# P.V. of four cross-attention heads in 512 columns, and the rotated queries turned one step earlier, in a decoder layer

## The reference

```python
scores = jnp.einsum('bqhgd,bkhd->bhgqk', q, k) * scale
attn = jax.nn.softmax(scores.astype(jnp.float32), axis=-1).astype(q.dtype)
out = jnp.einsum('bhgqk,bkhd->bqhgd', attn, v)
return out.reshape(b, q_len, N_HEADS * HEAD_DIM) @ Wo
```

## Time and profile before

| | us |
|---|---|
| median of 3 runs (1052.87 to 1053.89) | 1053.47 |
| the profiled execution | 1053.37 |
| its span | 1051.7 |
| TensorE busy | 1027.2 |
| DVE busy | 645.4 |
| ACT busy | 544.2 |
| POOL busy | 385.5 |

### The profile page before, as it was taken

How to read it: one execution, slowest core, us unless ns; L and a number is a source line. 1 busy time by engine, 2 the same in 40 slices (tenths; PEclk the granted TensorE clock), 3 DMA queues, 4 the chain that set the end, 5 groups by cost and what they waited for, 6 DMA issues and landing times.

```text
span 1051.7 us, 18418 instructions
## 1 busy us (share of the span) xinstructions
PE 1027.2 (98%) x6808; PEld 916.8 (87%) x6808; DVE 645.4 (61%) x1369; ACT 544.2 (52%) x1657; POOL 385.5 (37%) x370
## 2 busy tenths in 40 slices
PE   6999999999999999999999999999999999999997
PEld 5677777777889999999999999999999999799996
DVE  6788888887436555546545556555555575556554
ACT  5666666666526555536445446455545456522111
POOL 3544544544235324316224325225234236511110
PEclk9999999999999999999999999999999999999999
DMA  8300111105652003112022111121211013200000
GB/s 327 115 28 21 34 41 42 41 21 141 175 162 82 25 31 112 61 41 61 21 79 63 63 45 55 50 61 51 81 51 51 31 61 122 74 7 20 20 21 21
DMA packets 70114, 68.53 MB, mean 65 GB/s; under 512 B 3984, under 2 KB 53904, under 8 KB 70032
## 3 DMA queue, kind: packets, MB, share of 16 engines
q1 hardware_dynamic: 70032, 67.43, 20.5%
HBM read 48.55 MB, written 18.87 MB: 64 GB/s over the span
## 4 chain that ended last, share of the span: by engine, by line
PE 92%; DVE 4%; ACT 2%; issue 1%; DMA 1%; SPq 0%; POOLq 0%; POOL 0%; DVEq 0%; ACTq 0%
PE bank L218 27%; PE bank L220 26%; PE bank L219 26%; PE bank L945 5%; PE bank L729 2%; PE bank L689 1%; PE bank L693 1%; PE bank L699 1%; ACT Pb L1192 1%; DVE b_nb L1545 1%; PE bank L696 1%; DVE b_max L1542 1%; PE bank L611 1%; DMA rawKV<-in_L_attn_Wv_dram 1%; DVE PTal L1304 0%
## 5 line engine op out<-in xcount | busy, mean ns | idle before, releaser
L548 POOL TENSOR_TENSOR Pb<-Pb,b_rec 128x512 f32<-128x512 f32 x128 | 133.1, 1040 | 353.1 <-DVE b_rec L1549 352.7
L218 PE MATMUL bank<-XTh,WQh 128*128 128x256 f32 x512 | 145.9, 285 | 2.5 <-DVE Ql L1304 2.4
L220 PE MATMUL bank<-XTh,WQl 128*128 128x256 f32 x512 | 144.9, 283 | 0.0
L219 PE MATMUL bank<-XTl,WQh 128*128 128x256 f32 x512 | 144.8, 283 | 0.0
L1192 ACT ACTIVATE Pb<-bank,b_nb 128x256 f32<-128x256 f32 x256 | 119.0, 470 | 40.8 <-DVE b_nb L1545 40.1
L1304 DVE TENSOR_TENSOR Ol<-bank,Oh 128x256 fp32r<-128x256 f32 x128 | 54.0, 422 | 116.0 <-ACT Oh L1055 113.8
L1055 ACT ACTIVATE PTh<-bank 128x512 fp32r<-128x512 f32 x128 | 76.7, 599 | 85.3 <-PE bank L945 85.1
L1110 ACT ACTIVATE Pa<-bank,a_nb 128x128 f32<-128x128 f32 x256 | 90.4, 367 | 44.8 <-DVE a_nb L1425 44.8
L218 PE MATMUL bank<-WOh,Oh 128*128 128x512 f32 x256 | 110.0, 430 | 1.2 <-DVE x_res L1559 1.2
L510 POOL TENSOR_TENSOR Pa<-Pa,a_rec 128x512 f32<-128x512 f32 x64 | 68.2, 1066 | 104.6 <-DVE a_rec L1431 104.0
L218 PEld LDWEIGHTS bank<-XTh,WQh 128*128 128x128 f32 x512 | 97.7, 191 | 8.8 <-DVE Ql L1304 4.1
(11 more groups left out here) (230 smaller groups left out, 2865.0 us busy)
## 6 DMA issues: line engine op xcount, KB each, us to landing
kv_scratch<-KVst SPq DMA_DIRECT2D x64, 256.0 KB, 3.1
KV<-kv_scratch SPq DMA_DIRECT2D x32, 512.0 KB, 3.5
raw<-in_L_xattn_Wo_dram SPq DMA_DIRECT2D x32, 256.0 KB, 3.3
raw<-in_L_xattn_Wq_dram SPq DMA_DIRECT2D x24, 256.0 KB, 4.3
cx<-in_ctx_dram SPq DMA_DIRECT2D x8, 256.0 KB, 9.2
raw_first<-in_L_xattn_Wq_dram SPq DMA_DIRECT2D x8, 256.0 KB, 4.8
raw<-in_L_ffn_up_w_dram SPq DMA_DIRECT2D x8, 256.0 KB, 3.6
raw<-in_L_ffn_down_w_dram SPq DMA_DIRECT2D x8, 256.0 KB, 2.6
```

What stands on the lines that cost most here:

```text
L218: pe.matmul(dst, lh, rh, start=start, stop=False)
L219: pe.matmul(dst, lh, rl, start=False, stop=False)
L220: return pe.matmul(dst, ll, rh, start=False, stop=stop)
L548: gp.tensor_tensor(pk, pk, b_rec[:, k % 4, :].unsqueeze(2).to_broadcast([P, 2, KEYS]), ALU.mult).then_inc(b_g_norm, 1)
```

## The change

Cross-attention: `outputs` handles a quad, the two duos of an even and the following odd step (`QUADS` = 16 in a group, `QB` = 2 in a batch). `PTh` and `PTl` are laid out by key chunk, each with 512 columns of four heads. P.V. of a quad stands in the next even step between the scores and the transposes, and that of the last quad where P.V. of duo 31 stood. It waits for `PTl` of the quad's odd duo and for `Ol` of the quad before. ACT and DVE empty the whole bank 5 once per quad, at the beginning of the even step: ACT ahead of `PTh`, DVE behind the maxima and ahead of `PTl`. The counts that SP, `out_piece` and ACT's weight chunks wait for are changed to quads.

Self-attention: `turn_qk`, `qk_hi` and `qk_lo` are split. The queries' part stands in step 6 (on TensorE behind the transposes of step 6 and ahead of `values(5)`, on ACT and DVE at the end of step 6), the keys' part stays in step 7.

```diff
@@ SP group
-                            sp.wait_ge(b_pe_pv, DUOS * g + done)
+                            sp.wait_ge(b_pe_pv, QUADS * g + done // 2)
@@ TensorE
-            def turn_qk(b):
-
-                pe.wait_ge(v_qr, 2 * b + 2)
+            def turn_q(b):
+
+                pe.wait_ge(v_qr, 2 * b + 1)
...
+            def turn_k(b):
+
+                pe.wait_ge(v_qr, 2 * b + 2)
@@ TensorE batch
+                    if j == 6 and not last:
+                        turn_q(b + 1)
                     if j == 7 and not last:
-                        turn_qk(b + 1)
+                        turn_k(b + 1)
@@ TensorE out_piece
-                pe.wait_ge(b_v_o, DUOS * g + PB * b + i + 2)
+                pe.wait_ge(b_v_o, QUADS * g + QB * b + i // 2 + 2)
@@ TensorE outputs
-            def outputs(g, k):
-
-                pe.wait_ge(b_v_pt, DUOS * g + k + 3)
-                pe.wait_ge(b_v_o, DUOS * g + k + 1)
-                slot = (k // PB) % 3
+            def outputs(g, q):
+
+                pe.wait_ge(b_v_pt, DUOS * g + 2 * q + 4)
+                pe.wait_ge(b_v_o, QUADS * g + q + 1)
+                slot = (q // QB) % 3
                 for c in range(2):
...
-                    op = split3(pe, bank[5][:, 0:KEYS], vh, vl, PTh[:, k % 2, c * KEYS:(c + 1) * KEYS],
-                                PTl[:, k % 2, c * KEYS:(c + 1) * KEYS], c == 0, c == 1)
+                    op = split3(pe, bank[5][:], vh, vl, PTh[:, c, :], PTl[:, c, :], c == 0, c == 1)
@@ TensorE group
+                    if k and k % 2 == 0:
+                        outputs(g, k // 2 - 1)
 
                     pe.wait_ge(b_g_norm, DUOS * g + k + 1)
...
-                    if k:
-                        outputs(g, k - 1)
                 out_piece(g, NB - 1, 0)
-                outputs(g, DUOS - 1)
+                outputs(g, QUADS - 1)
@@ ACT batch
+                    if j == 6 and not last:
+                        q_hi(b + 1)
                 if not last:
-                    qk_hi(b + 1)
+                    k_hi(b + 1)
@@ ACT outputs
-                hi(Oh[:, b % 2, 2 * i:2 * i + 2, :],
-                   bank[5][:, 0:KEYS].rearrange("p (h n) -> p h n", h=2)).then_inc(b_a_o, 1)
+                hi(Oh[:, b % 2, 4 * i:4 * i + 4, :],
+                   bank[5][:].rearrange("p (h n) -> p h n", h=4)).then_inc(b_a_o, 1)
@@ ACT group
                 for k in range(DUOS):
-
+                    if k and k % 2 == 0:
+                        outputs(g, k // 2 - 1)
                     act.wait_ge(b_pe_pt, DUOS * g + k + 1)
-                    hi(PTh[:, k % 2, :], bank[3 + k % 2][:]).then_inc(b_a_pt, 1)
+                    hi(PTh[:, :, (k % 2) * KEYS:(k % 2 + 1) * KEYS],
+                       bank[3 + k % 2][:].rearrange("p (c n) -> p c n", c=2)).then_inc(b_a_pt, 1)
@@ DVE batch
+                    if j == 6:
+                        q_lo(b + 1)
                 if not last:
-                    qk_lo(b + 1)
+                    k_lo(b + 1)
@@ DVE group
+                    if k and k % 2 == 0:
+                        outputs(g, k // 2 - 1)
                     dve.wait_ge(b_a_pt, DUOS * g + k + 1)
-                    lo(PTl[:, k % 2, :], bank[3 + k % 2][:], PTh[:, k % 2, :]).then_inc(b_v_pt, 1)
+                    cols = slice((k % 2) * KEYS, (k % 2 + 1) * KEYS)
+                    lo(PTl[:, :, cols], bank[3 + k % 2][:].rearrange("p (c n) -> p c n", c=2),
+                       PTh[:, :, cols]).then_inc(b_v_pt, 1)
...
-                    if k:
-                        outputs(g, k - 1)
```

More of the change, by code:

```diff
@@ L52 @@
 PB = XG // 2
+QUADS = DUOS // 2
+QB = PB // 2
 INT, LAT, NE = 1024, 256, 8
@@ L832, in _ @@
             turn_weights(6)
-            turn_qk(0)
+            turn_q(0)
+            turn_k(0)
             unit(0, (2, 3))
@@ L1076, in values_hi, with q_hi, k_hi @@
                    bank[0][:, P:2 * P].rearrange("p (j d) -> p j d", j=SKV)).then_inc(a_v, 1)
-            def qk_hi(b):
+            def q_hi(b):
                 act.wait_ge(pe_qk, 2 * b + 1)
                 hi(QTh[:], bank[1][:].rearrange("p (k n) -> p k n", k=KC)).then_inc(a_qk, 1)
+            def k_hi(b):
                 act.wait_ge(pe_qk, 2 * b + 2)
@@ L1163, in _ @@
             weight_a(6)
-            qk_hi(0)
+            q_hi(0)
+            k_hi(0)
             act.wait_ge(v_c, 2)
@@ L1220, in _, with outputs @@
             hi(GTh[:, :, 0:NE], gate_raw[:]).then_inc(c_a_g, 1)
-            def outputs(g, k):
-                act.wait_ge(b_pe_pv, DUOS * g + k + 1)
-                if g == 0 and k == 0:
+            def outputs(g, q):
+                act.wait_ge(b_pe_pv, QUADS * g + q + 1)
+                if g == 0 and q == 0:
                     for slot in range(SLOTS):
                         act.wait_ge(st_u[slot], stored_in(slot, NU))
-                b, i = k // PB, k % PB
-                hi(Oh[:, b % 2, 2 * i:2 * i + 2, :],
-                   bank[5][:, 0:KEYS].rearrange("p (h n) -> p h n", h=2)).then_inc(b_a_o, 1)
+                b, i = q // QB, q % QB
+                hi(Oh[:, b % 2, 4 * i:4 * i + 4, :],
+                   bank[5][:].rearrange("p (h n) -> p h n", h=4)).then_inc(b_a_o, 1)
             def group(g, last):
@@ L1245, in split_weights @@
                             elif i == NUP + NFC:
-                                act.wait_ge(b_pe_pv, DUOS * g + 24)
+                                act.wait_ge(b_pe_pv, QUADS * g + 12)
                             else:
@@ L1389, in values_lo, with q_lo, k_lo @@
                 lo(vv[0], bank[0][:, P:2 * P].rearrange("p (j d) -> p j d", j=SKV), vv[1]).then_inc(v_vl, 1)
-            def qk_lo(b):
+            def q_lo(b):
                 dve.wait_ge(a_qk, 2 * b + 1)
                 lo(QTl[:], bank[1][:].rearrange("p (k n) -> p k n", k=KC), QTh[:]).then_inc(v_qkl, 1)
+            def k_lo(b):
                 dve.wait_ge(a_qk, 2 * b + 2)
@@ L1515, in _ @@
             weight_a(6)
-            qk_lo(0)
+            q_lo(0)
+            k_lo(0)
             dve.wait_ge(g_const, 9)
@@ L1593, in _, with outputs @@
             lo(GTl[:, :, 0:NE], gate_raw[:], GTh[:, :, 0:NE]).then_inc(c_v_g0, 1)
-            def outputs(g, k):
-                dve.wait_ge(b_a_o, DUOS * g + k + 1)
-                if g == 0 and k == 0:
+            def outputs(g, q):
+                dve.wait_ge(b_a_o, QUADS * g + q + 1)
+                if g == 0 and q == 0:
                     for slot in range(SLOTS):
                         dve.wait_ge(st_u[slot], stored_in(slot, NU))
-                b, i = k // PB, k % PB
-                lo(Ol[:, b % 2, 2 * i:2 * i + 2, :], bank[5][:, 0:KEYS].rearrange("p (h n) -> p h n", h=2),
-                   Oh[:, b % 2, 2 * i:2 * i + 2, :]).then_inc(b_v_o, 1)
+                b, i = q // QB, q % QB
+                lo(Ol[:, b % 2, 4 * i:4 * i + 4, :], bank[5][:].rearrange("p (h n) -> p h n", h=4),
+                   Oh[:, b % 2, 4 * i:4 * i + 4, :]).then_inc(b_v_o, 1)
             def group(g, last):
```

## The result

| | before | changed |
|---|---|---|
| median, us | 1053.43 | 1045.84 |
| range of 4 runs, us | 1052.87 to 1053.89 | 1045.18 to 1046.71 |
| the profiled execution, us | 1053.37 | 1046.71 |
| its span, us | 1051.7 | 1045.0 |

The account below looks back on a forecast made before the run. TensorE, busy 98% of the span, was taken to bound the kernel. Terms 3.4 + 2.1 - 0.9 + 1.7 + 3.1 = 9.4 us off 1053.4 gave 1044.0; term bounds 1041.8 to 1047.5, range with rivals 1041.5 to 1049.5.

Parts of the forecast that it names:

- P.V. in 512 columns: Cross-attention P.V. on TensorE: a pair takes 1.38 us instead of 1.44, over 64 pairs; 3.4 us gained.
- group starts: Cross-attention steps 0 to 3 of each group: TensorE's stall in step 2 shrinks from 0.80 to 0.29; 2.1 us gained.
- group ends: First three cross-attention groups: output piece 2 waits 0.3 us for the last P.V.'s low part; 0.9 us lost.
- last group from step 24: Last cross-attention group, where no Q remains: TensorE's standing falls from 3.0 to 1.3 us; 1.7 us gained.
- queries in step 6: Seven self-attention batches with a successor: query transposes fill TensorE's wait after T(6); 0.44 us each, 3.1 us gained.
- The Trainium skill's two prices: For P.V. matmuls: a gap formula gives 15 ns a pair, 1 us in all; sustained 131 ns would give 42 us.
- The wait for PTl in the steady steps: Cross-attention P.V. waiting for the odd duo's PTl: forecast not to occur, PTl ready 1.6 us after T, cover some 3.6.
- The slower rival: Steady cross-attention steps: PTl of the odd duo is late, 56 pairs standing 0.25 us cost 14, giving 1058; chance 0.05.
- The three waits for the low part of the output bank: Last group from step 24: TensorE waits like the 0.6 us around 906.25, forecast to go.
- the new 1.1 before the last batch's first piece: Last group, behind out of step 31: the next out waits for the residual, forecast at 1.0 us.
- the waits only move: Rival: cross-attention group starts and last group give nothing, group ends cost their 0.9; 1047.8 us, chance 0.17.
- TensorE's hole: Self-attention batch end: T(6) done at 119.35, values product starts only at 119.88 for PTal; query transposes should fill it.

Follow-up runs that it names:

- e3: The changed kernel with P.V. of a quad as 4 times 3 matmuls of 256 columns in place of 2 times 3 of 512; 1048.61 us.
- e4: The changed kernel with P.V. of each group's last quad ahead of the last batch's first output piece instead of behind it; 1043.85 us.
- e2: The kernel before with only the self-attention edits, the rotated queries in step 6; 1049.95 us.
- e6: The changed kernel without b_nb: maximum negated in the reduction, score scale put into the key weights at the start; 1047.78 us.
- e9: The changed kernel with each group's last P.V. before the output piece and no b_nb, score scale in the key products' copy out of the bank; 1041.18 us.
- e7: The changed kernel with only TensorE's query transposes in step 6, ACT's QTh and DVE's QTl behind step 7 again; 1048.86 us.

## Why the prediction was right or wrong

The time, 1045.84, lies within the forecast's own range of 1041.8 to 1047.5; the gain of 7.6 is 1.8 short of 9.4. (The slow end of that range was added up wrongly: the lowest values that the terms were given, 3.0, 1.2, -1.2, 0.9 and 0, make 3.9 us and 1049.5.) Term by term:

| term | forecast, us | measured, us | from |
|---|---|---|---|
| P.V. in 512 columns | 3.4 | 2.9 | 1.440 and 1.394 a pair, x 64; e3 |
| group starts | 2.1 | 1.7 | distances of steps 0 to 3 |
| group ends | -0.9 | -0.96 | 3 x 0.32; e4 |
| last group from step 24 | 1.7 | 0.25 | stalls of 2.98 before, 2.74 after |
| queries in step 6 | 3.1 | 3.0 | 7 x 0.42; e2 |

- **P.V. width.** The mechanism was right; the distance from start to start is 0.232 in this place, not the 0.230 of the stretch in the earlier trace rows. The Trainium skill's two prices (TensorE: Matmul & The Clock Gate, Back-to-back issue gap) do not hold for these matmuls: where its formula makes 15 ns a pair, the rows have 46.
- **The wait for PTl in the steady steps.** It did not appear: steps alternate between 3.99 and 5.37 us, 9.36 a pair where it was 9.41. The slower rival is out.
- **Group starts.** Second to fourth group as walked: the stall of 0.80 went, and P.V. of step 2 stands 0.21 and 0.10. In the first group a second one appeared that the walk had not: step 4 stands 0.35 because b_nb of step 3 ran 1.27 us behind a POOL weight part. So the 0.6 forecast for that group became 0.2.
- **The last group.** This is the term that failed. The three waits for the low part of the output bank and the 1.3 for the residual did go, and the new 1.1 before the last batch's first piece came as forecast (1.27 in place of 0.23). But at step 30, where 0.3 was written, stand 1.16, and 0.46 at step 26, where nothing was. Both are PTl behind a blocked b_nb; the walk had put POOL's weight parts elsewhere by some tenths. The rival "the waits only move" was therefore right for the last group (2.98 against 2.74) and wrong for the group starts. e6 and e9 show the cause by taking the operation away: 3.2 us in cross-attention, 1.3 of it in the last group, where 1.45 were missing.
- **Queries in step 6.** Right in size, and its reasons hold: values(6) came forward, 0.18 and 0.10 were given back at values(7) (0.15 to 0.25 forecast), and the projection starts 0.42 earlier from batch to batch. e7 shows that the half of the reason that carries the gain is ACT's and DVE's, not TensorE's hole.

The terms add up to 6.9. In the two traces cross-attention is 4.25 shorter and the seven batches 2.96, 7.2 in all; the 0.3 between is spread over steps too small to read. Against it stand the 1.57 of the lower clock in batch 0, and 1.1 that this execution's start was shorter: 6.7, the difference of the spans.

## What to carry to other kernels

When a stage is priced by walking the queues, a place where two engines start within a few hundredths of a microsecond is not one number but two, and the range should hold both; here such a place was worth 0.87 us. A tiny operation that can be blocked should not stand in a queue ahead of the one on which the bottleneck engine waits: removing it (a negation in the reduction, a scale in a copy that happens anyway) gained 3.2 us, while moving it behind, together with the maximum that it scales, cost 9.9. And of a hole in the bottleneck engine ask what the next wait is bound to, since filling it alone can give nothing.

## What the runs showed of the hardware

- The DVE operation b_nb, which scales 128 x 2 elements from SBUF to SBUF, takes 0.17 us or 1.31, by whether it starts 0.01 us before or after a GpSimd operation of 1.29 us. The maximum over 128 x 512 elements of a bank is not stretched by a GpSimd operation (0.69 us at most, 48 cases).
- The first matmul after a wait costs 0.10 us more than its columns do when it has 512 (0.336 against 0.231), where the forecast had 0.08.
- TensorE's granted clock fell to the 1.2 GHz level for over 3.2 us early in batch 0 in six of twelve profiled executions, behind the same 1.64 us of standing that the other six have, and cost 1.5 to 1.6 us.
- Twelve query matmuls of 256 columns take 1.423 us in some builds and 1.432 to 1.438 in others, with no edit to them. It is worth 1 us over the kernel; its cause stays open.
